# Second attention in steps of two head pairs, with a borrowed score bank and the values' bank for projections

## What is computed

```python
def _L1_xattn_ref(q, k, v, w_q, w_k, w_v, w_o):      # H = 16 heads, D_K = D_V = 64
    b, n, _ = q.shape
    qh = (q @ w_q.T).reshape(b, n, H, D_K).transpose(0, 2, 1, 3)
    kh = (k @ w_k.T).reshape(b, n, H, D_K).transpose(0, 2, 1, 3)
    vh = (v @ w_v.T).reshape(b, n, H, D_V).transpose(0, 2, 1, 3)
    scores = jnp.einsum('bhid,bhjd->bhij', qh, kh) / math.sqrt(D_K)
    causal = jnp.tril(jnp.ones((n, n), dtype=bool))
    attn = jax.nn.softmax(jnp.where(causal[None, None], scores, -jnp.inf), axis=-1)
    out = jnp.einsum('bhij,bhjd->bhid', attn, vh)
    return out.transpose(0, 2, 1, 3).reshape(b, n, H * D_V) @ w_o.T
...
x = x + _L0_xattn_ref(_layernorm(x), ctx_1024, ctx_1024, mask, mask, ...)
x = x + _L0_ffn_ref(_layernorm(x), ...)
x = x + _L1_xattn_ref(_layernorm(x), ctx_1024, ctx_1024, ...)
x = x + _L1_ffn_ref(_layernorm(x), ...)   # 8 experts, top 2, gated by silu
```

## Time and profile before

| | |
|---|---|
| median of 3 runs | 683.18 us (681.15 to 685.83) |
| the profiled execution | 682.42 us, span 680.6 us |
| busy share of the span | PE 91%, PEld 69%, DVE 64%, ACT 53%, POOL 51% |
| second attention, first scores to the epilogue's first turn | 286.26 to 565.65 us |

### The profile page before, as it was taken

One profiled execution on the slowest core, in us unless ns is written; L12 is line 12 of the kernel. 1 busy time (PEld: TensorE's weight loads), 2 busy tenths in 40 slices (PEclk: granted clock), 3 DMA queues, 4 the chain that ended last, 5 costly groups with the idle time before them and its releaser, 6 DMA issues.

```text
span 680.6 us, 15610 instructions
## 1 busy us (share of the span) xinstructions
PE 616.7 (91%) x5150; PEld 468.5 (69%) x5169; DVE 438.9 (64%) x1158; ACT 363.9 (53%) x978; POOL 344.7 (51%) x518
## 2 busy tenths in 40 slices
PE   6889999998888998799999999999999988999970
PEld 3555666564477998576868687777777756788970
DVE  6778898998453443466676766667665884734445
ACT  3167777776433333476565657576665653333440
POOL 6140555544366675144445647474655575545650
PEclk8999999999889999999999999999999999999995
DMA  9944033501315542500000000000000005175636
GB/s 283 392 195 166 18 152 154 222 14 32 109 59 176 176 132 82 171 24 0 26 1 28 13 28 14 5 14 1 17 1 13 5 17 161 57 213 143 156 94 185
DMA packets 42004, 63.80 MB, mean 94 GB/s; under 512 B 5646, under 2 KB 30484, under 8 KB 39606
## 3 DMA queue, kind: packets, MB, share of 16 engines
q1 hardware_dynamic: 35094, 52.66, 24.2%
q0 software_dynamic: 4544, 8.44, 3.6%
q10 hardware_dynamic: 2288, 1.70, 0.8%
HBM read 35.08 MB, written 28.62 MB: 94 GB/s over the span
## 4 chain that ended last, share of the span: by engine, by line
PE 76%; DVE 12%; issue 4%; DMA 4%; ACT 2%; POOL 1%; SPq 1%; DVEq 0%; POOLq 0%
PE ps L796 13%; PE ps L832 9%; PE ps L881 7%; PE ps L934 5%; PE ps L946 5%; PE ps L959 4%; PE ps L529 4%; PE ps L589 4%; PE ps L921 3%; PE ps L557 3%; PE ps L919 3%; PE ps L895 3%; PE ps L497 3%; PE ps L949 2%; PE ps L905 2%
## 5 line engine op out<-in xcount | busy, mean ns | idle before, releaser
L1269 ACT ACTIVATE work<-ps,nb 128x128 f32<-128x128 f32 (+1 forms) x256 | 104.3, 420 | 30.6 <-DVE nb L1814 24.8
L2081 POOL DMA_INDIRECT results<-ye,dsti x78 | 76.7, 984 | 55.1 <-issue 17.3
L2099 POOL TENSOR_TENSOR work<-work,rc 128x256 f32<-128x256 f32 x64 | 39.2, 612 | 122.3 <-DVE rc L1822 122.3
L796 PE MATMUL ps<-ex,w_up 128*128 128x256 f32 (+3 forms) x480 | 96.6, 347 | 3.5 <-ACT ex L1191 2.4
L1426 DVE TENSOR_REDUCE work<-ps 128x4 f32<-128x1024 f32 x64 | 78.3, 1223 | 15.5 <-PE ps L563 14.0
L2017 POOL DMA_INDIRECT dispatch<-pay,sloti x64 | 65.3, 1021 | 40.8 <-DVE sloti L1504 24.5
L796 PEld LDWEIGHTS ps<-ex,w_up 128*128 128x128 f32 (+1 forms) x480 | 74.8, 187 | 13.1 <-ACT ex L1191 3.6
L1115 ACT ACTIVATE work<-ps 128x1024 f32<-128x1024 f32 x64 | 65.6, 1024 | 27.9 <-PE ps L557 26.0
L1807 DVE TENSOR_REDUCE mx<-ps 128x6 f32<-128x768 f32 x64 | 60.9, 952 | 29.8 <-PE ps L921 29.6
L1829 DVE COPY work<-ps 128x768 f32<-128x768 f32 x64 | 61.1, 955 | 25.7 <-PE ps L934 25.6
L832 PE MATMUL ps<-w_dn,ht 128*128 x546 | 70.8, 279 | 3.9 <-DVE ye L1729 2.0
(11 more groups left out here) (179 smaller groups left out, 1198.4 us busy)
## 6 DMA issues: line engine op xcount, KB each, us to landing
dispatch<-w_up SPq DMA_DIRECT2D x16, 1096.5 KB, 6.8
w_up<-in_wgu SPq DMA_DIRECT2D x24, 352.0 KB, 3.4
w_up<-in_w SPq DMA_DIRECT2D x24, 256.0 KB, 3.0
xt<-dispatch SPq DMA_DIRECT2D x30, 129.0 KB, 2.6
ct<-in_ctxT SPq DMA_DIRECT2D x16, 128.0 KB, 2.5
w_dn<-in_w SPq DMA_DIRECT2D x1, 2048.0 KB, 9.9
ybuf<-results SPq DMA_DIRECT2D x16, 128.0 KB, 2.2
work<-results SPq DMA_DIRECT2D x8, 256.0 KB, 4.8
```

Source lines behind the costliest of these rows:

```text
L796: return pe.matmul(ps[0:f, bank, c0:c0 + n], w, ex[:, u % 2, 0:n], start=True, stop=True)
L1269: ac = act.activation(p1[:, pp % 2, e, cols], bk[:, cols], ACT.Exp, scale=SC1, bias=nb1[:, pp % 2, e, t:t + 1], accum_out=rs1[:, pp % 2, e ...
L2081: po.indirect_dma_start(yc[l], bass.IndirectOffsetOnAxis(ap=dsti[:, u % 8, n:n + 1], axis=0), ye[:, k, n, :], None, bounds_check=TOPK * T ...
```

## The change

The order of the second attention is written anew on all engines, in four steps of two head pairs each. A step q (0, 2, 4, 6) is on TensorE: masks q and q+1, scores q and q+1, mixes q-4 and q-3, turn q-2, one to two pieces, turn q-1, further pieces (or the output projection, in step 2). The pieces are shared between three banks: bank 7, bank 1 (a score bank, free from the exponentials of pair q until the masks of pair q+2), and bank 6 (free from `take_out1` until the next mix). `transpose_x` goes to bank 1 and `output1` to bank 6. Guards are put before masks and mixes: the masks of a step wait until ScalarE has copied the piece out of bank 1, the mixes until it has copied that out of bank 6. p1 gets four buffers, two of them in sg, which only the expert part uses; so the exponentials of pair n wait for the turn of pair n-4 and no longer for that of n-2. On ScalarE `take_out1` stands between the two pairs' exponentials and all copies of pieces stand behind both. On VectorE both row maxima come first; `combine` (old `enter1`'s first half) moves from step 1 to step 2, `norm_in` and the statistics to other steps, and the two halves of `first_table` from steps 1 and 3 to the ends of steps 2 and 4. On GpSimd the inverse roots and the context's split are done up to three pairs later. The number of matmuls and of copies is the same.

Buffers and output projection:

```diff
-        p1 = work[:, 12288:13824].rearrange("p (r h n) -> p r h n", r=2, h=2)
...
+        p1 = [half_of[:, 3 * 2 * P * r:3 * 2 * P * (r + 1)].rearrange("p (h n) -> p h n", h=2)
+              for half_of in (sg[:, :, :, :].rearrange("p r c n -> p (r c n)"), work[:, 12288:13824]) for r in range(2)]
...
+            def output1(b, free, bank=7):
+                if free:
+                    pe.wait_ge(*free)
                 pe.wait_ge(*after(1, "pv_evac", 4 * no(b) + 4))
...
+                        mm = pe.matmul(ps[:, bank, t * P:(t + 1) * P], ot1[:, k, t * P:(t + 1) * P], wo1[:, k, :],
```

TensorE's `body1`:

```diff
+                def mix_at(p):
+                    for r in (p, p + 1):
+                        if r >= 0:
+                            mix1(b, r, first)
+                        elif behind:
+                            mix1(d, M1 + r, False)
+
+                def turn_at(p):
+                    if p >= 0:
+                        turn1(b, p, first)
                     elif behind:
-                        mix1(d, 5 + p, False)
-
-                    if first and p == 0:
-                        project1_after(b, 7, qk(b, 5), 4)
-                    if ahead:
-                        if p == 0:
-                            project1_after(c, 0, after(1, "x_split", no(c) + 1))
-                        elif p in (1, 2):
-                            project1_after(c, 2 * p, qk(c, 2 * p))
-                        elif p == 3:
-                            project1_after(c, 5, after(1, "x_add", 2 * no(d) + 2) if behind else qk(c, 5))
-                        elif p == 4:
-                            project1_after(c, 7, qk(c, 7))
-                        elif p == 5:
-                            values1(c, 1, vv(c, 1))
-                    if p == 6 and behind:
-                        transpose_t2(1, d, vv(c, 3) if ahead else None)
-
-                    if p >= 2:
-                        if first and p == 2:
-                            pe.wait_ge(*qk(b, 8))
-                        turn1(b, p - 2, first)
-                    elif behind:
-                        turn1(d, 6 + p, False)
+                        turn1(d, M1 + p, False)
+
+                def scored(p):
+                    return (s["s_exp"], 8 * no(b) + p + 1)
+
+                if not first:
+                    pe.wait_ge(*vv(b, 2))
+                masks1(b, 0, first)
+                masks1(b, 1, first)
+                scores1(b, 0, first)
+                if no(b) >= 2:
+                    prefix(1, d2, None)
+                scores1(b, 1, first)
+                if first:
+                    project1(b, 6, 6)
+                    project1_after(b, 7, qk(b, 5), 4)
+                else:
+                    pe.wait_ge(*vv(b, 3))
+                mix_at(-4)
+                turn_at(-2)
+                if ahead:
+                    project1_after(c, 0, vv(b, 4))
+                    project1_after(c, 1, scored(0), 1)
+                turn_at(-1)
+                if ahead:
+                    values1(c, 0, after(1, "pv_evac", 4 * no(d) + 3) if behind else qk(b, 7), 6)
+                    project1_after(c, 2, qk(c, 1))
+
+                if ahead:
+                    pe.wait_ge(*qk(c, 2))
+                masks1(b, 2, first)
+                masks1(b, 3, first)
+                scores1(b, 2, first)
+                scores1(b, 3, first)
+                if ahead:
+                    pe.wait_ge(*vv(c, 1))
+                mix_at(-2)
+                if first:
+                    pe.wait_ge(*qk(b, 8))
+                turn_at(0)
+                if ahead:
+                    project1_after(c, 3, qk(c, 3))
+                    transpose_x(1, c, scored(2), 1)
+                turn_at(1)
+                if behind:
+                    output1(d, None, 6)
+
+                if ahead:
+                    pe.wait_ge(*after(1, "x_split", no(c) + 1))
+                masks1(b, 4, first)
+                masks1(b, 5, first)
+                scores1(b, 4, first)
+                scores1(b, 5, first)
+                if behind:
+                    pe.wait_ge(*after(1, "x_add", 2 * no(d) + 2))
+                mix_at(0)
+                turn_at(2)
+                if ahead:
+                    project1_after(c, 4, qk(c, 4))
+                    project1_after(c, 5, scored(4), 1)
+                turn_at(3)
+                if ahead:
+                    project1_after(c, 6, after(1, "pv_evac", 4 * no(b) + 1), 6)
+                if behind:
+                    transpose_t2(1, d, qk(c, 5) if ahead else vv(b, 4))
+
+                if ahead:
+                    pe.wait_ge(*qk(c, 6))
+                masks1(b, 6, first)
+                masks1(b, 7, first)
+                scores1(b, 6, first)
+                scores1(b, 7, first)
+                if behind:
+                    logits(1, d, None)
+                if ahead:
+                    pe.wait_ge(*qk(c, 7))
+                mix_at(2)
+                turn_at(4)
+                if ahead:
+                    project1_after(c, 7, after(1, "t2_evac", no(d) + 1) if behind else qk(c, 5))
+                    values1(c, 1, scored(6), 1)
+                turn_at(5)
+                if ahead:
+                    values1(c, 2, after(1, "pv_evac", 4 * no(b) + 2), 6)
+                    values1(c, 3, qk(c, 8))
```

ScalarE:

```diff
                 act.wait_ge(s["s_nb"], n + 1)
                 if not (first and pp < 2):
-                    act.wait_ge(s["pt_psum"], n - 1)
                     act.wait_ge(s["s_rec"], n - 1)
+                if not (first and pp < 4):
+                    act.wait_ge(s["pt_psum"], n - 3)
...
+                exps1(b, 0, first)
+                if first:
+                    qk_out(b, 6, 6)
+                else:
+                    take_out1(d, 2)
+                exps1(b, 1, first)
+                if first:
+                    qk_out(b, 7, 4)
+                if ahead:
+                    qk_out(c, 0)
+                    qk_out(c, 1, 1)
+                    v_out(c, 0, 6)
+                    qk_out(c, 2)
+
+                exps1(b, 2, first)
+                if behind:
+                    take_out1(d, 3)
+                exps1(b, 3, first)
+                if ahead:
+                    qk_out(c, 3)
+                    x_high(1, c, 1)
+
+                exps1(b, 4, first)
+                take_out1(b, 0, first)
+                exps1(b, 5, first)
+                if ahead:
+                    qk_out(c, 4)
+                    qk_out(c, 5, 1)
+                    qk_out(c, 6, 6)
+                if behind:
+                    t2_out(1, d)
+
+                exps1(b, 6, first)
+                take_out1(b, 1)
+                exps1(b, 7, first)
+                if ahead:
+                    qk_out(c, 7)
+                    v_out(c, 1, 1)
+                    v_out(c, 2, 6)
+                    v_out(c, 3)
```

VectorE's `body1`:

```diff
+                if no(b) >= 2:
+                    place(1, d2, (0,))
+                row_max1(b, 0, first)
+                row_max1(b, 1, first)
+                if behind:
+                    pt_out(d, 6, False)
+                recip1(b, 0, first)
+                if no(b) >= 2:
+                    place(1, d2, (1,))
+                if behind:
+                    pt_out(d, 7, False)
+                recip1(b, 1, first)
+                if ahead and behind:
+                    norm_in(1, c)
+
+                row_max1(b, 2, first)
+                row_max1(b, 3, first)
+                pt_out(b, 0, first)
+                recip1(b, 2, first)
+                pt_out(b, 1, first)
+                if more:
+                    combine(0, off(b, 2))
+                recip1(b, 3, first)
+                if no(b) == B - 1:
+                    first_table(1, 0)
+                if ahead:
+                    x_low(1, c, 1)
+                if behind:
+                    attend1(d, 6)
+                    stats(1, d, 1)
+
+                row_max1(b, 4, first)
+                row_max1(b, 5, first)
+                pt_out(b, 2, first)
+                recip1(b, 4, first)
+                if behind:
+                    norm_out(1, d)
+                pt_out(b, 3, first)
+                recip1(b, 5, first)
+                if more:
+                    stats(1, off(b, 2), 0)
+                if no(b) == B - 1:
+                    first_table(1, 1)
+
+                row_max1(b, 6, first)
+                if behind:
+                    choose(1, d, (0, 1))
+                row_max1(b, 7, first)
+                if behind:
+                    choose(1, d, (2, 3))
+                pt_out(b, 4, first)
+                recip1(b, 6, first)
+                pt_out(b, 5, first)
+                recip1(b, 7, first)
```

133 lines of the change are left out of this document (19 added, 114 removed).

## The result

The changed kernel takes 676.86 us (median; 674.52 to 678.69), the kernel before 684.34 on the same chip (680.38 to 686.97). The ratio is 0.9906, with a 95% interval of 0.988 to 0.9931. The forecast was 677.4 us in a range of 668 to 688. The profiled execution has a span of 673.2 us against 680.6, so 7.4 us less.

A forecast was written before the change was run, and what follows sets the result against it. TensorE's queue was taken to bound batches 1 to 6, the chain between engines batch 0 and the last. Six middle batches -8.9, batch 0 +2.2, last +0.9 gave -5.8 us: 677.4, range 668 to 688.

The forecast's parts named there:

- Form changes, the main term: TensorE, per two pairs: three changes of matmul tile form gone, 0.2 + 0.21 + 0.17 = 0.58 us, or 2.3 per batch.
- The chain, step 4: Middle batches: masks wait for ScalarE's copy out of bank 1, so step 4 takes 7.88 us, 0.64 of it waiting.
- The other steps: Middle batches: step 0 takes 8.53 us, step 2 9.83, step 6 8.44; with step 4 the sum is 34.68.
- a sign to look for: Sign of being right: the second pair's scores 0.64 us behind the first's, no idle weight load between them.
- The combining pass: VectorE's `combine`: 1.26 us; if it collides with GpSimd, step 2 is 1.0 longer in batch 0, 0.3 in others: 679.9.
- Batch 0: First batch: +2.2 us; exponentials from about 287.2, step 2 set by VectorE at 9.0, step 4 7.88, step 6 8.04.
- one of the signs of being wrong: Sign against the forecast: a granted clock under 1.00.
- So I price no loss of clock: TensorE's clock: waits of up to 0.64 us don't come near the 2.08 that left it at 1.00.
- Last batch: Last batch: +0.9 us; `first_table`'s second half (2.2) delays pair 6's row maxima by 1.45; epilogue's first turn at 10.1.
- TensorE as the bound of every step: Rival, chance 0.17: copies free bank 1 before TensorE asks; middle batches go to 33.0, the kernel to 667 us.
- Longer copies: Rival, chance 0.21: ScalarE's copies 0.71 us apart; steps 0 and 4 grow by 0.4, batch 0 by 1: 683.5, no change.
- ScalarE blocked between its exponentials: Rival, chance 0.15: `take_out1` waits for late mixes; 1 us over the margin in three steps of seven batches gives 698.

## Why the prediction held, and where it missed

**Form changes, the main term: the cause is right, the account incomplete.** 0.58 was forecast for three changes per two pairs. Putting two of them back costs 0.35 where nothing else moves (step 2), which fits, and in time it gives the whole gain back. The price is not the same everywhere: 0.35, 0.81 and twice nothing, 1.16 per middle batch, since each step has another limit. That is less than the 2.06 by which the middle batches became shorter, and the rest was not taken apart by a run. One piece of it the forecast passed over. It says that nothing but the form changes is removed, 2.3 per batch, yet its own sum for TensorE's queue falls by 3.2 (36.16 to 33.0). In the kernel before, the first mix of batches 2 to 6 also waited for VectorE's copy:

```profile
389.87 0.20 PEld L946 LDWEIGHTS ps<-work 128*64 128x64 f32 x4 [0.73 <-DVE work L1829]
```

where a form change alone leaves 0.33. In the changed kernel it is 0.33 in that place too, so some 0.4 per batch went with this wait (an estimate, the difference of the two).

**The chain, step 4: right.** 7.88 forecast, 7.79 measured, waits of 0.64 and 0.61. One run lengthened the chain by 1.04 and one shortened it by 0.14, and the step followed by 1.03 and 0.14; the same passes in step 2 moved nothing.

**The other steps: right in kind, long by 0.1 to 0.2.** 8.53, 9.83 and 8.44 forecast, 8.34, 9.77 and 8.20 measured. In step 0 `prefix` was put at 0.5 and costs 0.36 (from the first scores to the mixes it is 1.87, and 1.51 in step 2), and the maxima begin 1.23 after the scores and not 1.45, so the copy that the last piece waits for comes earlier. The second pair's scores begin 0.76 behind the first's in step 2, where 0.64 was a sign to look for. In step 6 the second half of `choose` was put at 0.72 and holds VectorE for 0.32:

```profile
382.35 0.18 DVE L1521 TENSOR_TENSOR hot<-cf,topi 128x32 bf16<-128x32 f32 x1
382.56 0.17 DVE L1528 TENSOR_TENSOR hots<-hot 128x16 bf16<-128x16 bf16 x1
382.67 0.96 DVE L1884 COPY work<-ps 128x768 f32<-128x768 f32 x1
```

so its copy ends at 5.37 after the scores and not at 5.80, and the second turn doesn't wait. Six batches at 34.68 are 208.1 us, and 204.4 were measured. (The gain was forecast from 36.16 six times; batch 1 took 35.80 before, so the two gains differ by 3.2 and not by 3.7.) The turns of step 2 stand 1.99 apart by their weight loads, forecast 1.97.

**The combining pass: no collision in the changed kernel.** In batches 0 to 5, which have it, its four passes take 1.25 to 1.27. In batch 2 they run from 367.44 to 368.71, between GpSimd's pass for pair 2, which ends at 367.31, and that for pair 3, which begins at 369.01. The rule of the Trainium skill (SBUF — State Buffer, Who interferes with whom) didn't strike there. It struck elsewhere: in the table, where I hadn't looked, and in this same pass once I had moved it behind the reciprocal in batch 0 (2.22 and 2.23).

**Batch 0: the right sum from two wrong terms.** +2.2 forecast, +2.35 measured. The exponentials began at 286.79 and not 287.2, and step 2 took 8.76 and not 9.0. Step 4 took 8.63 in place of 7.88, at a clock of 0.80, one of the signs of being wrong that the forecast named. "So I price no loss of clock" is the step that failed: 2.08 us was the longest wait in the second attention before and left the clock at 1.00, but batch 0 now has a wait of 2.75:

```profile
301.22 0.61 PE L906 MATMUL ps<-cbi 128*128 128x256 bf16 x4 [2.75 <-DVE hl L1467]
```

My own numbers for batch 0 had it: step 2 at 9.0, where its terms for TensorE (scores, two turns, piece, transposition, masks) add up to 4.4. The premise was weak too. Elsewhere in the trace of before, and in the changed kernel ahead of batch 0's first scores, the clock is at its lower level behind waits of no more than 1.10 and 1.09 (these rows are of the kernel before and of the changed one):

```profile
182.00:184.50 2.50, 2.50 (x12) 1.32 (x16) 0.00 (x0) 0.00 (x0) 0.30 (x2) 0.50 0.63 178
282.00:284.00 2.00, 2.00 (x12) 1.38 (x11) 0.83 (x6) 1.10 (x2) 1.17 (x3) 0.50 0.52 151
```

**Last batch: the term was mis-sized.** +0.9 forecast, +2.9 measured. The place was right, the second half of the table ahead of row maximum 6, and the whole miss is in the step from there on, 12.17 for 10.1. The 2.2 us for the table came from the trace of before, where GpSimd's passes ended at 549.62, just after its first operation began. Moved behind a reciprocal, an operation in its middle fell beside both passes and the table took 3.6; the maxima came 3.65 after the scores, where the forecast had 2.45 (1.00 and a delay of 1.45). TensorE then stood for 3.76, and what followed ran at half speed at first. The next two windows are from 550 to 558:

```profile
550.00:554.00 4.00, 0.94 (x10) 0.64 (x6) 3.73 (x16) 2.39 (x11) 0.00 (x0) 1.00 0.32 68
554.00:558.00 4.00, 3.29 (x24) 2.55 (x26) 1.95 (x6) 1.43 (x8) 2.23 (x4) 0.57 0.82 232
```

**The rivals.** TensorE as the bound of every step is refuted by step 4, though steps 2 and 6 are its own. Longer copies: they are 0.51 apart also where they read PSUM in a row. ScalarE blocked between its exponentials: `take_out1` waits for nothing in any middle step.

## What to carry to other kernels

Write down what limits each step, then test it with a dummy pass in that step and the same pass in a step that should hide it. Read the result from the step's length in the trace, which repeats here to 0.02 us, where the timed ratios can't tell 0.4%. Before a batch of small VectorE operations is moved, see what the instruction ahead of it releases on GpSimd: put them ahead of the release. Where a change makes TensorE wait longer, price the clock too, or fill the wait; that a long wait elsewhere left the clock alone proves little.

## What the hardware showed that I had not expected

- A VectorE operation on 5 numbers took 0.15 us alone and 1.83 beside GpSimd's two passes, which took their usual 0.62 and 1.05. It had started 0.19 us before them and still ended with them. A scalar minimum on 8 numbers (1.66 in place of 0.16) and a maximum of two elements (0.94) ended with them too, and four combining passes took 2.23 in place of 1.25. Two normalisations of 128x128, begun 0.16 us before such passes, took 0.87 together, and 0.60 without the passes beside them (283.71), so they lost 0.27 and not a whole pass. Why some are held to the end and others not stays open.
- TensorE's granted clock fell to its lower level (0.50, 1.2 GHz) behind waits of 3.76, 2.75 and 2.20 us, but also behind one of 1.53 (the split first in batch 0) and, with two buffers, in step 6 of each of batches 2 to 6 behind waits of 1.67 to 1.94. The 0.57 to 0.80 above are means of windows that hold both levels. It did not fall every time: the kernel with one bank has a batch with waits of 2.06, 2.26 and 2.20 at 1.00 throughout, and behind a wait of 1.89 us it stayed at 1.00 in one execution and was 0.50 for 2.8 us in another. So the longest wait alone doesn't tell, and what does stays open. Six matmuls on zeros in the wait kept it at 1.00 in batch 0, in both executions seen.
- Three chips differed by 4% in the whole kernel and by 0.02 us or so in a middle batch's steps. Where the slow one loses was not looked into.
